# Splitting x and W by ScalarE's conversion instead of a VectorE mask, with the variance's constant in the Sqrt's bias, in a graph layer with LayerNorm on one core

## The reference

```python
Wi, Wj = (W[:, :Din], W[:, Din:])
mi = jnp.einsum('bkd,od->bko', x, Wi)
mj = jnp.einsum('bkd,od->bko', x, Wj)
a = adj.astype(x.dtype)
deg = a.sum(axis=1)
out = deg[None, :, None] * (mi + b) + jnp.einsum('ij,bjo->bio', a, mj)
...
x = _layernorm(x + _L0_gnn_ref(x, adj, L0_gnn_W, L0_gnn_b), axis=-1)
```

## Time and profile before

| what | value |
| --- | --- |
| median of 3 runs | 1643.62 us (1643.59 to 1643.74) |
| the profiled execution | 1643.72 us, its span 1641.9 us |
| TensorE busy | 1634.2 us of the span, 7196 matmuls |
| weight loads (PEld) | 1346.8 us |
| VectorE / ScalarE / GpSimd busy | 844.8 / 661.7 / 498.4 us |
| granted TensorE clock | 0.999 of full speed |
| bytes moved | 187.27 MB |

### The profile page before, as it was taken

The page is one execution under the profiler, slowest core; times in us unless marked ns, Lnnn a source line. Parts: engine busy times, 40 slices in busy tenths (PEclk is TensorE's granted clock), DMA queues, the critical chain, the costliest instruction groups (busy, mean ns, idle before and its releaser), DMA issues.

```text
span 1641.9 us, 24654 instructions
## 1 busy us (share of the span) xinstructions
PE 1634.2 (100%) x7196; PEld 1346.8 (82%) x7196; DVE 844.8 (51%) x1879; ACT 661.7 (40%) x964; POOL 498.4 (30%) x386
## 2 busy tenths in 40 slices
PE   9999999999999999999999999999999999999998
PEld 6888888888888888888888888888888888888886
DVE  8787644554444544444544544444544454544544
ACT  5765445332453324532245332452325522255221
POOL 3532134311343114431144211442114421144210
PEclk9999999999999999999999999999999999999999
DMA  6676422332234323243223332233323333233332
GB/s 205 193 226 223 141 84 94 131 108 96 83 102 133 100 93 96 89 134 109 84 95 101 123 115 83 95 114 117 102 83 102 124 106 106 74 101 115 96 115 70
DMA packets 102843, 187.27 MB, mean 114 GB/s; under 512 B 11424, under 2 KB 11680, under 8 KB 102816
## 3 DMA queue, kind: packets, MB, share of 16 engines
q1 hardware_dynamic: 84672, 154.05, 29.1%
q10 hardware_dynamic: 18144, 32.91, 6.3%
HBM read 119.80 MB, written 67.11 MB: 114 GB/s over the span
## 4 chain that ended last, share of the span: by engine, by line
PE 98%; DVE 1%; DMA 0%; issue 0%; POOL 0%; ACT 0%; DVEq 0%
PE agg_ps L375 57%; PE cross_ps L343 14%; PE main_ps L351 14%; PE main_ps L353 14%; DVE W_lo L558 0%; DVE W_df L561 0%; DMA mi_in<-in_wt 0%; DVE adjT L555 0%; DVE x_raw L579 0%; DVE mj_lo L568 0%; PE deg_ps L360 0%; POOL x_df L281 0%; DVE x_top L576 0%; DVE stats L630 0%; DVE r L628 0%
## 5 line engine op out<-in xcount | busy, mean ns | idle before, releaser
L375 PE MATMUL agg_ps<-mj_hi,adjT 128*128 128x512 f32 x2048 | 797.0, 389 | 0.0
L375 PE MATMUL agg_ps<-mj_lo,adjT 128*128 128x512 f32 x2048 | 796.7, 389 | 0.0
L470 ACT ACTIVATE adjT<-adjT 128x2048 fp32r (+1 forms) x128 | 245.4, 1917 | 562.8 <-PE agg_ps L375 562.8
L375 PEld LDWEIGHTS agg_ps<-mj_hi,adjT 128*128 128x128 f32 x2048 | 384.5, 188 | 79.9
L375 PEld LDWEIGHTS agg_ps<-mj_lo,adjT 128*128 128x128 f32 x2048 | 384.3, 188 | 79.7
L351 PE MATMUL main_ps<-W_hi,x_hi 128*128 128x512 f32 x1008 | 392.3, 389 | 0.0
L353 PE MATMUL main_ps<-W_lo,x_lo 128*128 128x512 f32 x1008 | 392.1, 389 | 0.0
L292 POOL TENSOR_TENSOR mi_in<-mi_in,bias 128x512 f32<-128x512 f32 x128 | 166.9, 1307 | 649.9 <-DMA mi_in<-mi_dram 649.9
L628 DVE TENSOR_TENSOR r<-agg_ps,r 128x512 f32<-128x512 f32 x128 | 88.6, 692 | 355.0 <-PE agg_ps L375 354.9
L343 PE MATMUL cross_ps<-W_df,x_df 128*128 128x512 f32 x1008 | 270.2, 390 | 0.6 <-DVE W_df L561 0.5
L286 POOL TENSOR_TENSOR mj_lo<-mj,mj_hi 128x512 f32 (+1 forms) x126 | 166.7, 1323 | 323.4 <-ACT mj_hi L458 323.4
(11 more groups left out here) (59 smaller groups left out, 592.1 us busy)
## 6 DMA issues: line engine op xcount, KB each, us to landing
mi_dram<-mi SPq DMA_DIRECT2D x128, 256.0 KB, 2.1
mi_in<-mi_dram SPq DMA_DIRECT2D x128, 256.0 KB, 2.7
r<-in_x SPq DMA_DIRECT2D x128, 256.0 KB, 2.6
out<-r SPq DMA_DIRECT2D x127, 256.0 KB, 2.1
x_raw<-in_xt ACTq DMA_DIRECT2D x124, 256.0 KB, 2.7
adj_in<-in_adjt SPq DMA_DIRECT2D x64, 256.0 KB, 3.9
r<-in_wt SPq DMA_DIRECT2D x4, 256.0 KB, 5.2
adj_in<-in_xt SPq DMA_DIRECT2D x2, 256.0 KB, 4.0
```

What stands on the lines that cost most here:

```text
L375: last = nc.tensor.matmul(agg_ps[s][:, :], adjT[s][:, j, :], part[:, j, :], start=(j == 0 and part is mj_hi), stop=(j == NT - 1 and part i ...
L470: nc.scalar.activation(adjT[s][:, :, :], adjT8[:, :, bass.ds(i * P, P)], ACT.Copy).then_inc(adjT_ready, 1)
```

## The change

The mask is gone. ScalarE converts x_raw straight to x_hi (round_x) and each W chunk straight to W_hi (round_w); VectorE subtracts that result from the unsplit values (rest_of_x, split_w), and ScalarE's scaling follows as a step of its own (scale_x). x_top remains only as a place to load one W chunk (w_spare); GpSimd's difference reads x_hi in its place. In a projection tile n ScalarE now runs round_x(n+1), take_cross(n, 0), scale_x(n+1), and VectorE runs rest_of_x(n+1) before combine_mj(n), where split_x(n+2) stood behind it. For this VectorE's loop over a batch's groups has its first and last group written out. The x of a batch's second tile is still split in the aggregation of the batch before, with VectorE's part now there too. All conversions of W come before the two native_mi. The Sqrt reads the variance and adds 1e-5 itself, from a tile eps that GpSimd sets; it waits for one step less. var_eps is still computed, for the Newton step.

```diff
-        x_top = sb("x_top", [P, D], fp32)
+        w_spare = sb("w_spare", [P, D], fp32)
...
+        eps = sb("eps", [P, 1], fp32)
...
-        w_stage = [r[0], r[1], r[2], r[3], mi_in[0], mi_in[1], x_top, mi]
-        scratch = [adjT8[:, 2 * q:2 * q + 2, N // 2:N].bitcast(fp32) for q in range(NT // 2)]
-        w_top = scratch
+        w_stage = [r[0], r[1], r[2], r[3], mi_in[0], mi_in[1], w_spare, mi]
...
         def _(pool):
             pool.memset(warm[:, :], 0.0).then_inc(zeroed, 1)
             pool.memset(ones[:, :].bitcast(fp32), 1.0).then_inc(zeroed, 1)
+            pool.memset(eps[:, :], EPS).then_inc(zeroed, 1)
 
             def difference(n, s):
                 pool.wait_ge(x_parts_ready, 2 * (n - NATIVE) + 2)
-                pool.tensor_tensor(x_df[s][:, :], x_top[:, :], x_lo[s][:, :].bitcast(fp32),
+                pool.tensor_tensor(x_df[s][:, :], x_hi[s][:, :].bitcast(fp32), x_lo[s][:, :].bitcast(fp32),
                                    ALU.subtract).then_inc(x_df_ready, 1)
...
         def _(act):
-            def copy_w_hi(c, order):
-                act.wait_ge(w_top_ready, order + 1)
-                nc.scalar.activation(halves(W_hi[:, c, :]), w_top[order], ACT.Copy).then_inc(w_hi_ready, 1)
+            def round_w(c):
+                act.wait_ge(w_loaded[c], 16)
+                nc.scalar.activation(W_hi[:, c, :], w_stage[c][:, :], ACT.Copy).then_inc(w_hi_ready, 1)
...
-            def parts(n, s):
-                act.wait_ge(x_top_ready, n - NATIVE + 1)
+            def round_x(n, s, turn):
+                act.wait_ge(x_loaded[s], turn)
                 if not (known(n) and n < NATIVE + 2):
                     act.wait_ge(main_done, 2 * n - 2)
-                nc.scalar.activation(x_hi[s][:, :], x_top[:, :], ACT.Copy).then_inc(x_parts_ready, 1)
+                nc.scalar.activation(x_hi[s][:, :], x_raw[s][:, :], ACT.Copy).then_inc(x_parts_ready, 1)
+
+            def scale_x(n, s):
                 act.wait_ge(x_rest_ready, n - NATIVE + 1)
                 nc.scalar.activation(x_lo[s][:, :], x_raw[s][:, :], ACT.Copy, scale=S).then_inc(x_parts_ready, 1)
...
             def root(m):
-                act.wait_ge(ln_step, LN * m + 3)
-                nc.scalar.activation(std[:, :], var_eps[:, :], ACT.Sqrt).then_inc(std_ready, 1)
+                act.wait_ge(ln_step, LN * m + 2)
+                nc.scalar.activation(std[:, :], mean_var[:, 1:2], ACT.Sqrt, bias=eps[:, :]).then_inc(std_ready, 1)
 
             act.dma_start(w_stage[DK][:, :], wt[DK]).then_inc(w_loaded[DK], 16)
-            for order in range(DK):
-                copy_w_hi(DK + order, order)
+            for c in range(DK, 2 * DK):
+                round_w(c)
+            round_w(0)
             native_mj_hi(0)
-            copy_w_hi(0, DK)
+            round_x(NATIVE, 0, 16)
+            round_w(1)
             native_mj_hi(1)
-            parts(NATIVE, 0)
+            scale_x(NATIVE, 0)
             load_x(NATIVE + 2, 0)
+            for c in range(2, DK):
+                round_w(c)
             native_mi(0)
-            for order in range(1, DK):
-                copy_w_hi(order, DK + order)
             native_mi(1)
...
-                        if not (final and last_group and u == GT - 1) and (zero or not (known(g) and t == 0)):
-                            parts(n + 1, (u + 1) % 2)
+                        next_x = not (final and last_group and u == GT - 1) and (zero or not (known(g) and t == 0))
+                        if next_x:
+                            round_x(n + 1, (u + 1) % 2, 16 * (NP * bt + 2 * g + (u + 1) // 2))
                         take_cross(n, 0)
+                        if next_x:
+                            scale_x(n + 1, (u + 1) % 2)
                         if not (final and last_group and u >= GT - 3):
                             load_x(n + 3, (u + 1) % 2)
...
                         if i == NT - 1:
-                            parts(NT + 1, 1)
+                            round_x(NT + 1, 1, 16 * NP)
+                            scale_x(NT + 1, 1)
                         root(i)
...
             def split_w(c, order):
-                top = w_top[order]
-                dve.wait_ge(w_loaded[c], 16)
-                nc.vector.tensor_scalar(top.bitcast(u32), halves(w_stage[c][:, :]).bitcast(u32),
-                                        HI_BITS, None, ALU.bitwise_and).then_inc(w_top_ready, 1)
-                dve.wait_ge(w_top_ready, order + 1)
-                nc.vector.tensor_tensor(halves(W_lo[:, c, :]), halves(w_stage[c][:, :]), top,
+                dve.wait_ge(w_hi_ready, order + 1)
+                nc.vector.tensor_tensor(W_lo[:, c, :], w_stage[c][:, :], W_hi[:, c, :].bitcast(fp32),
                                         ALU.subtract).then_inc(w_lo_ready, 1)
                 dve.wait_ge(w_lo_ready, order + 1)
-                nc.vector.scalar_tensor_tensor(halves(W_df[:, c, :]), top, 1.0 / S,
-                                               halves(W_lo[:, c, :]).bitcast(fp32),
+                nc.vector.scalar_tensor_tensor(W_df[:, c, :], W_hi[:, c, :].bitcast(fp32), 1.0 / S,
+                                               W_lo[:, c, :].bitcast(fp32),
                                                ALU.mult, ALU.subtract).then_inc(w_ready, 1)
...
-            def split_x(n, s, turn):
-                dve.wait_ge(x_loaded[s], turn)
-                if not (known(n) and n == NATIVE):
-                    dve.wait_ge(x_parts_ready, 2 * (n - NATIVE))
-                    dve.wait_ge(x_df_ready, n - NATIVE)
-                nc.vector.tensor_scalar(x_top[:, :].bitcast(u32), x_raw[s][:, :].bitcast(u32),
-                                        HI_BITS, None, ALU.bitwise_and).then_inc(x_top_ready, 1)
-                dve.wait_ge(x_top_ready, n - NATIVE + 1)
-                nc.vector.tensor_tensor(x_raw[s][:, :], x_raw[s][:, :], x_top[:, :],
+            def rest_of_x(n, s):
+                dve.wait_ge(x_parts_ready, 2 * (n - NATIVE) + 1)
+                nc.vector.tensor_tensor(x_raw[s][:, :], x_raw[s][:, :], x_hi[s][:, :].bitcast(fp32),
                                         ALU.subtract).then_inc(x_rest_ready, 1)
...
-            split_x(NATIVE, 0, 16)
+            rest_of_x(NATIVE, 0)
             for order in range(1, DK):
                 split_w(order, DK + order)
-            split_x(NATIVE + 1, 1, 16)
...
+                        if not (final and known(g) and g == NG - 1 and u == GT - 1) and (zero or not (known(g) and t == 0)):
+                            rest_of_x(n + 1, (u + 1) % 2)
                         combine_mj(n)
-                        if not (final and known(g) and g == NG - 1 and u >= GT - 2):
-                            split_x(n + 2, u % 2, 16 * (NP * bt + 2 * g + u // 2 + 1))
...
-                over_groups(dve, zero, final, proj)
+                if zero:
+                    for g in range(NG):
+                        proj(g)
+                else:
+                    proj(0)
+                    with dve.Fori(1, NG - 1) as g:
+                        proj(g)
+                    proj(NG - 1)
...
                         if not ending:
                             residual(m + 1, i + 1, (u + 1) % GT, 16 * (NG * bt + g + 1 + (u + 1) // GT))
+                        elif not final:
+                            rest_of_x(base + NT + 1, 1)
                         normalise(m, u, u % 2, final and ending)
```

More of the change, by code:

```diff
@@ L10, in bass_adj_resnorm @@
     i32 = mybir.dt.int32
-    u32 = mybir.dt.uint32
     i8 = mybir.dt.int8
@@ L32, in bass_adj_resnorm @@
     EPS = 1e-5
-    HI_BITS = 0xFFFFF000
     S = 4096.0
@@ L103, in bass_adj_resnorm @@
         x_loaded = [sem(f"x_loaded{s}") for s in range(2)]
-        x_top_ready = sem("x_top_ready")
         x_rest_ready = sem("x_rest_ready")
@@ L541, in batch @@
                         if i == 1 and not final:
-                            parts(NT * bt + NT + 1, 1)
+                            round_x(NT * bt + NT + 1, 1, 16 * (NP * bt + NP))
+                            scale_x(NT * bt + NT + 1, 1)
                         root(NT * bt + NT - 2 + i)
```

3 lines of the change are left out of this document (removed).

## The result

The changed kernel takes **1646.34 us** in the median of 22 runs (1642.67 to 1649.24), the kernel before 1643.68 in 22 runs beside it (1643.48 to 1644.35). The ratio is 1.0015, 95% interval 1.0008 to 1.0021: 2.7 us slower, within the 0.2%, but outside the range of the prediction. The runs of the kernel before lie within 0.9 us, those of the changed one within 6.6, so something in it seems to happen in most runs, in different strength, and not in the fastest.

What follows compares the result with a forecast made beforehand. TensorE, holding 98% of the span, was taken as the bound. From 1643.72, gains of 0.87, 0.45, 0.24 and 0.12, costs of 0.1 and 0.1, and 0.1 to the median gave 1642.14, stated as 1642.1 us; range 1641.6 to 1643.3.

Steps and rivals of the forecast that it cites:

- The split of W (head): At the start: last W_df ends at 19.4 to 19.8, mi(1) at 20.1, before TensorE needs them; gain 0.87 us.
- x_df of the second split tile: Projection tile n=3: x_df ready at 23.45, at worst 23.8, TensorE arriving at 23.62; gain 0.45 us, less 0 to 0.2.
- The stall at 34.16: Early projection: TensorE's wait for mi goes because the store of mi(2) comes 3.4 us earlier; gain 0.24 us.
- Every other projection tile: x_df slack falls from 2.72 to 1.6 us, less behind a widen; TensorE still covered; cost 0.1 us.
- The end: Last tile's normalisation: Sqrt starts 0.19 us earlier, its bias operand costs 0.07 us; gain 0.12 us.
- the first part: What bounds the kernel: TensorE's early waits, 1.56 us, and the last normalisation; gains possible nowhere else.
- worth nothing, since it idles: Every other tile: freeing VectorE of 126 masks of 0.42 us gains nothing.
- Rival C: Every projection: longer chain makes TensorE wait for x_df; one GpSimd hold 1.3 us; with 0.4 us queue 1659; chance 0.03.
- Rival B: Batch 0 projection: small new stalls, 0.1 us in each of 14 tiles, 1.4 us, giving 1643.5; chance 0.05.

Runs made afterwards that it cites:

- w_only: The kernel before with only the new split of W (ScalarE converts, VectorE subtracts): 1642.47 us.
- pad56: The changed kernel with 56 one-column VectorE fills of an unused buffer added in batch 0's projection: 1642.53 us.
- old_root: The changed kernel with the old Sqrt of var_eps, without a bias operand: 1646.65 us.
- deg_later: The changed kernel with TensorE's degrees(3) placed before row tile 12 instead of 11: 1643.2 us.
- busy8b: pad56 with its fills into w_spare, plus one 128x240 VectorE addition in row tile 8: 1644.12 us.
- w_pad98b: w_only with seven fills a tile, their buffer declared last, to move VectorE's next pause into row tile 8: 1646.13 us.
- before_busy: The kernel before with one 128x240 VectorE addition in row tile 8 of batch 0, between last count and residual: 1647.6 us.
- chunks_early: The changed kernel with adjacency chunks dealt out 4,4,4,3,3,3,3,3,3,3,3 instead of 2,3,3,3,3,3,3,4,4,4,4: 1643.29 us.
- res_first: The changed kernel with the residual of row tile 8 of batch 0 ahead of that tile's four counts: 1647.11 us.

## Why the prediction was wrong

**The split of W (head): right.** The last W_df ended at 19.18 (forecast 19.4 to 19.8; the meeting with GpSimd made one W_lo 0.6 us longer, where 1.0 to 1.3 was allowed for), mi(1) at 19.74 (20.1); both stalls are gone:

```profile
18.49 0.69 DVE L559 SCALAR_TENSOR_TENSOR W_df<-W_hi,W_lo 128x512 fp32r<-128x512 f32 x1
...
19.14 0.60 ACT L429 ACTIVATE mi<-cross_ps 128x512 f32<-128x512 f32 x1 [2.32 <-DMA mi_dram<-mi]
...
21.73 1.30 POOL L274 TENSOR_TENSOR x_df<-x_hi,x_lo 128x512 fp32r<-128x512 f32 x1 [5.15 <-ACT x_lo L440]
...
24.04 0.87 PEld L336 LDWEIGHTS cross_ps<-W_df,x_df 128*128 128x128 f32 x4
```

w_only, with this part alone, is 1.2 us under the kernel before.

**x_df of the second split tile: right.** It ended at 23.03, a microsecond ahead of its first load, without a wait.

**The stall at 34.16: right**, no wait for mi is left. In all, TensorE is 0.97 us ahead at 50 us, where 1.56 was forecast; 0.37 of the rest arose at 5 us, where the unsplit tiles' matmuls began that much later than in the profile of before; in pad56's they began 0.06 later, so I don't lay it on the change. About 0.2 us are left over in both (pad56 is 1.27 ahead).

**Every other projection tile: right in its terms.** x_df has 1.73 us of slack in an ordinary tile (forecast 1.6) and 0.86 behind a widen (0.8); behind the widen of batch 0 the wait of 0.3 us costs 0.26, forecast 0 to 0.2, because GpSimd's difference, begun behind a count of VectorE, took 1.61 us there instead of 1.3. TensorE never waits for x_df again and again.

**The end: right.** The Sqrt starts 0.04 us behind the variance and takes 276 ns in the median instead of 203:

```profile
1640.34 0.30 ACT L469 ACTIVATE std<-mean_var,eps 128x1 f32<-128x1 f32 x1 [6.96 <-DVE mean_var L624]
```

The operand costs 73 ns, where I took 70. The Trainium skill, "ScalarE: Activation LUTs", section "What ACT_TABLE_LOAD costs", has 93; the measurement decides. From the last sum to the end of the chain it is 3.68 us instead of 3.78: 0.10 gained, 0.12 forecast.

**The step that failed** is in the first part: "From there to the end TensorE waits for nobody [...] whatever the others do", and with it "it can lose in every tile, if it makes x_df later". That TensorE had no wait was true. That nothing but x_df could give it one was taken without a look. deg_part was ready 0.17 us before TensorE wanted it, and the residual of row tile 8 started 0.13 us before the bias addition; what the change does to VectorE's order in time in the row tiles was put at nothing ("worth nothing, since it idles"), and what the runs showed there is 1.8 us of wait for deg_part and 1.6 us of slow clock. Rival C named the hold between VectorE and GpSimd and its 1.3 us, but only for the difference of x in the projection. Rival B looked for small stalls in batch 0's projection tiles, not in its row tiles. The pause could not be seen in the profile of before as a cost; the missing cover could. VectorE's addition of the aggregate waited 0.8 us for TensorE in row tile 6 of the kernel before, and in row tile 8 it followed the residual at once:

```profile
148.00 0.69 DVE L628 TENSOR_TENSOR r<-agg_ps,r 128x512 f32<-128x512 f32 x1 [0.80 <-PE agg_ps L375]
...
163.02 0.69 DVE L628 TENSOR_TENSOR r<-agg_ps,r 128x512 f32<-128x512 f32 x1
```

With the race won the forecast holds: pad56, all of the change and 56 fills, without the stall, has 1642.53 against 1642.1, inside the range, and its span is 1.2 us shorter than before's.

**Still open.** Why the store takes 4 us. In all six profiles with a held residual (after, old_root, deg_later, busy8b, w_pad98b, before_busy) it took 3.5 to 4.1 us, in the others 2.0 to 2.5. In those six a 16 KB instruction packet (queue q8, 1.3 to 1.7 us) starts 0.8 to 1.1 us after the store is issued (in the changed kernel at 168.0); in all others it starts 2.0 us or more after the issue (in the kernel before at 169.5, when the store had landed). That this is the reason is argued, not shown: no run moves the packet by itself, and the next store takes 4.0 to 4.4 us in the same six without one, by then beside the late chunk loads. Open too are what the pause is, and why five kernels (after, old_root, deg_later, chunks_early, res_first) spend 2.2 us outside their span and all others 1.8. It isn't the written-out loop, which peeled tests:

> The kernel before with VectorE's loop over the projection groups of batches 1 to 5 written as first group, loop, last group, as in the kernel after; no operation added or removed. Theory 1 (the 0.35 us more outside the span comes with this form of the loop): time outside the span 2.15 instead of 1.8 us, median 1643.9 to 1644.1. Theory 2 (it comes with the new operations of the x split): 1.8 us and 1643.6. In neither case a wait for deg_part in batch 0, since the operations up to there and their places are those of before.

peeled has 1.80 us outside the span.

## What to carry to other kernels

A list of waits shows who is late, not who is nearly late. Before an engine's schedule is moved in a kernel where another engine never waits, look up the slack of each thing that engine waits for, in the stretch where the moved engine is busiest, and the order in which VectorE and GpSimd start operations on two SBUF tiles: here 0.17 and 0.13 us decided over almost 4. If a measurement scatters more after a change than before, look for a race first, and put new buffers behind the old ones when you test it.

## What I had not expected of the hardware

- VectorE pauses 0.36 us at a fixed place of its instruction stream, without a semaphore (operation 200 in four kernels, 314 in two), and 56 more instructions ahead of it take the pause out of row tile 8. In pad56, where it falls in a row tile with slack, TensorE doesn't wait for it; the profile shows it only as an unusual spacing, with an 8 KB instruction packet 0.9 to 1.7 us behind the start of the late operation.
- A short wait of TensorE cost about as much again. Behind waits of 2.0 to 2.7 us (four profiles) the clock stood at 1.2 GHz for 3.4 us, which cost 1.6 us in the changed kernel; behind one of 2.9 us (before_busy) for 6.8 us, about 2.8 us (14 weight loads spaced 0.43 us instead of 0.23). Behind one of 1.0 us (res_first) it stayed.
- Moving buffers by 192 bytes made each matmul of the projection some 2 ns longer (391 to 392 instead of 389 to 390), 6.5 us in all.
